# Causal selects of both attentions moved to GpSimd, and half-width scores for the second key block

## The reference, cut to what matters

```python
x = L0_attn_x                                  # (8, 256, 256)
xn = _layernorm(x)
s = mla(xn)                                    # q, k of 16 + 64 per head, rope, causal softmax
#   attn = einsum('bhqd,bhkd->bhqk', q, k) * SCALE;  attn + triu(-inf, k=1);  softmax;  @ v
f = ffn(xn)                                    # mha with 16 per head, the same mask, then
#   x = xn + h @ Wo.T;  + moe(rmsnorm(x)), top 2 of 8 experts
out = x + s * silu(f)
```

## Time and profile before

| | before |
|---|---|
| median of 3 runs | 969.01 us (966.42 to 970.13) |
| the profiled execution | 961.99 us, of which the span from first to last instruction is 960.2 us |
| PE / DVE / ACT / POOL busy | 87% / 68% / 52% / 30% |
| mean granted TensorE clock | 0.952 of full speed |
| one batch of the loop | 77.4 to 77.6 us |

### The profile page before, as it was taken

How to read it: one execution, slowest core, us unless ns; L and a number is a source line. 1 busy time by engine, 2 the same in 40 slices (tenths; PEclk the granted TensorE clock), 3 DMA queues, 4 the chain that set the end, 5 groups by cost and what they waited for, 6 DMA issues and landing times.

```text
span 960.2 us, 20067 instructions
## 1 busy us (share of the span) xinstructions
PE 836.7 (87%) x6688; PEld 747.9 (78%) x6688; DVE 655.9 (68%) x2335; ACT 502.4 (52%) x1091; POOL 285.3 (30%) x282
## 2 busy tenths in 40 slices
PE   5879999999999998999999999977179999999980
PEld 3868988887887797797898788865169999998980
DVE  4877667667767857866866766763237777777754
ACT  2435365365356356446536535634047777676751
POOL 5520310330221131041032023001314565645641
PEclk9988999999999999999999999988579999999995
DMA  9000000000000000000000000030146677779836
GB/s 277 1 1 1 13 1 25 14 1 13 12 11 2 23 11 2 22 12 1 23 12 1 13 16 7 13 141 15 36 151 184 183 238 202 224 232 334 248 49 186
DMA packets 40159, 70.88 MB, mean 74 GB/s; under 512 B 10946, under 2 KB 35138, under 8 KB 37122
## 3 DMA queue, kind: packets, MB, share of 16 engines
q1 hardware_dynamic: 29074, 57.39, 17.7%
q0 software_dynamic: 9856, 12.13, 6.5%
q10 hardware_dynamic: 1152, 0.49, 0.3%
HBM read 55.25 MB, written 14.81 MB: 73 GB/s over the span
## 4 chain that ended last, share of the span: by engine, by line
PE 51%; DVE 14%; DMA 14%; issue 14%; POOL 3%; ACT 2%; SPq 1%; DVEq 0%; POOLq 0%; ACTq 0%
PE ps L575 40%; DMA expert_rows<-yo,slot_of 11%; PE ps L668 6%; PE ps L705 3%; DVE ps L1400 2%; DVE ps L1403 2%; POOL expert_rows L552 1%; DVE negm L1403 1%; PE ps L601 1%; DMA ln<-in_w_ln 1%; DVE negm L1400 1%; POOL xg L541 1%; PE ps L610 1%; DMA xg<-x_normalised,slot_of 1%; PE ps L805 1%
## 5 line engine op out<-in xcount | busy, mean ns | idle before, releaser
L1094 ACT ACTIVATE ex<-ps 128x384 f32<-128x384 f32 x256 | 125.2, 494 | 130.4 <-PE ps L575 128.9
L575 PE MATMUL ps<-qt,kt 128*128 128x256 f32 (+1 forms) x768 | 163.8, 324 | 4.5 <-issue 3.2
L505 POOL TENSOR_TENSOR tok<-tok,swp 128x256 f32<-128x256 f32 x128 | 97.2, 760 | 219.3 <-DVE swp L1355 218.3
L1400 DVE CUSTOM_DVE_ANT_0 ps<-ps,mask 128x128 f32<-128x128 f32 x256 | 76.2, 298 | 70.4 <-PE ps L575 42.6
L1403 DVE CUSTOM_DVE_ANT_0 ps<-ps,mask 128x256 f32<-128x256 f32 x256 | 118.5, 463 | 0.7
L575 PEld LDWEIGHTS ps<-qt,kt 128*128 128x128 f32 x768 | 109.3, 193 | 11.9 <-issue 7.0
L1234 DVE TENSOR_TENSOR wel<-raw,weh 128x768 fp32r<-128x768 f32 x92 | 88.1, 958 | 34.4 <-ACT weh L962 34.4
L552 POOL DMA_INDIRECT expert_rows<-yo,slot_of x46 | 77.9, 1693 | 104.7 <-DMA expert_rows<-yo,slot_of 54.8
L575 PE MATMUL ps<-wh,xth 128*128 128x320 f32 (+2 forms) x352 | 95.5, 353 | 5.9 <-DVE wl L1234 3.3
L1351 DVE TENSOR_TENSOR tok<-ps,cos_t 128x320 f32<-128x320 f32 x128 | 62.7, 490 | 52.3 <-PE ps L575 46.4
L962 ACT ACTIVATE qt<-ps 128x512 f32<-128x512 f32 (+1 forms) x96 | 57.0, 594 | 61.3 <-PE ps L668 54.6
(11 more groups left out here) (164 smaller groups left out, 1965.8 us busy)
## 6 DMA issues: line engine op xcount, KB each, us to landing
raw<-in_w_experts SPq DMA_DIRECT2D x23, 1536.0 KB, 7.2
mla_branch<-s_b SPq DMA_DIRECT2D x8, 256.0 KB, 2.1
expert_rows<-xn SPq DMA_DIRECT2D x8, 256.0 KB, 2.2
x_normalised<-otk SPq DMA_DIRECT2D x8, 256.0 KB, 2.1
xr<-in_x SPq DMA_DIRECT2D x1, 2048.0 KB, 14.8
s_tok<-mla_branch SPq DMA_DIRECT2D x1, 2048.0 KB, 14.2
w_cols_raw<-in_w_cols SPq DMA_DIRECT2D x1, 1792.0 KB, 15.6
x<-expert_rows SPq DMA_DIRECT2D x3, 512.0 KB, 5.1
```

Of the source, the lines that this page charges most:

```text
L505: nc.gpsimd.tensor_tensor(t, t, swp[:, n % 2, :, :], ALU.add).then_inc(tokd, 1)
L575: return nc.tensor.matmul(o, a, m, start=start, stop=stop, skip_group_check=True, **k)
L1094: nc.scalar.activation(ex[:, h % (2 * G), :], ps[4 + h % 2][:, P:4 * P], ACT.Exp, scale=scale).then_inc(ex_, 1)
L1400: nc.vector.tensor_tensor_reduce(out=o[:, 0:P], in0=o[:, 0:P], in1=mask2[:, 1, :], scale=-1.0, scalar=-2.0 * BIG, op0=ALU.add, op1=ALU.min ...
```

## The change

Masking leaves DVE and PE and goes to POOL, for both attentions. POOL runs `affine_select` in place on the same 256 columns of `ex`, once per head: it keeps a value where the query is not before the key and writes 0 elsewhere. `values(g)` of T2 now waits on POOL (`exm2`). `scores2` computes the second key block for queries 128 to 255 alone, and its two mask matmuls go. `power2(b-1)` stands after the select of head 6 in T1, and the four scatters of b-1 stand one each after the selects of heads 9, 10, 11 and 12 of T2. The tiles `seen`, `idb`, `maskb` and the two constants loaded for them go, with two small copies on ACT.

```diff
-            def scatter_slots(r):
-                pool.wait_ge(posd, r + 1)
-                pool.nop(nofuse=True)
-                for t in range(2):
-                    for k in range(2):
-                        nc.gpsimd.indirect_dma_start(slot[:, :], ...
+            def scatter_slot(r, t, k):
+                if t == 0 and k == 0:
+                    pool.wait_ge(posd, r + 1)
+                    pool.nop(nofuse=True)
+                nc.gpsimd.indirect_dma_start(slot[:, :], ...
+            def causal(b, ex_, exm, after):
+                for h in range(H):
+                    wait(pool, ex_, 16 * b + h + 1)
+                    pool.nop(nofuse=True)
+                    a = ex[:, h % (2 * G), 0:2 * P].rearrange("p (a q) -> p a q", a=2)
+                    nc.gpsimd.affine_select(a, a, [[0, 2], [1, P]], ALU.is_ge, zero, 0, -1).then_inc(exm, 1)
+                    after.get(h, lambda: None)()
+            def slots_between(r):
+                return {9 + 2 * t + k: lambda t=t, k=k: scatter_slot(r, t, k) for t in range(2) for k in range(2)}
+            zero = nc.gpsimd.to_reg(0.0)
+            causal(0, ex1, exm1, {})
             rope_sums(1)
+            causal(0, ex2, exm2, {})
             pool.wait_ge(s_slot, 16)
             with pool.Fori(1, last) as b:
-                power2(b - 1)
+                causal(b, ex1, exm1, {6: lambda: power2(b - 1)})
                 rope_sums(b + 1)
-                scatter_slots(b - 1)
-            power2(last - 1)
-            scatter_slots(last - 1)
+                causal(b, ex2, exm2, slots_between(b - 1))
+            causal(last, ex1, exm1, {6: lambda: power2(last - 1)})
+            causal(last, ex2, exm2, slots_between(last - 1))
             power2(last)
...
             def scores2(h, o):
-                mm(o[:, 0:2 * P], kt2[:, h // 2, P:S], qt2[:, h, :], True, False)
-                mm(o[:, 2 * P:4 * P], kt2[:, h // 2, 0:P], qt2[:, h, :], False, False)
-                mm(o[:, P:2 * P], idb[:, :], maskb[:, :], False, True)
-                return mm(o[:, 2 * P:3 * P], idb[:, :], maskb[:, :], False, True)
+                mm(o[:, P:2 * P], kt2[:, h // 2, P:S], qt2[:, h, P:S], True, True)
+                return mm(o[:, 2 * P:4 * P], kt2[:, h // 2, 0:P], qt2[:, h, :], True, True)
...
-                heads(b, scores2, st2, ex2, ex2, pv2, ov2, v2, ...
+                heads(b, scores2, st2, ex2, exm2, pv2, ov2, v2, ...
...
-            def causal(b, h):
-                wait(dve, ex1, 16 * b + h + 1)
-                a = ex[:, h % (2 * G), 0:2 * P].rearrange("p (a q) -> p a q", a=2)
-                nc.vector.tensor_tensor(a, a, seen[:, 0:1, :].broadcast_to([P, 2, P]), ALU.min).then_inc(exm1, 1)
             def stage_m2(b, after):
                 for h in range(H):
-                    causal(b, h)
                     maxima(b, h, (h % 2) * (H // 2) + h // 2, negm2, m2d, mx2)
```

More of the change, by code:

```diff
@@ L56 @@
 BIG = -1e30
-BOUND = 1e30
 IT = FF // P
@@ L92, in build @@
 def build(nc, x, w_cols, w_dq, w_uqr, w_dkv, w_ukv, w_out, w_o, w_ln1, w_ln2, w_r, w_experts,
-          cosines, sines, ident, mask, mask_t, seen_t, upper, route_c, slots, out):
+          cosines, sines, ident, mask, upper, route_c, slots, out):
     ctx = ExitStack()
@@ L171, in build @@
         kt = sb("kt", [P, H, S], F32, early)
-        seen = sb("seen", [P, 1, P], F32, late)
-        idb = sb("idb", [P, P], BF16, late)
-        maskb = sb("maskb", [P, P], BF16, late)
         mask2 = sb("mask2", [P, 2, P], BF16, late)
@@ L513, in power2 @@
                 nc.gpsimd.tensor_tensor(rstd2[:, :], msq2[:, :], mhalf[:, 0:2], ALU.pow).then_inc(rm2, 1)
-            def scatter_slots(r):
-                pool.wait_ge(posd, r + 1)
-                pool.nop(nofuse=True)
-                for t in range(2):
-                    for k in range(2):
-                        nc.gpsimd.indirect_dma_start(slot[:, :], bass.IndirectOffsetOnAxis(posu[:, t, k:k + 1], 0),
-                                                     meta[:, t, k, :], None).then_inc(msc, 16)
+            def scatter_slot(r, t, k):
+                if t == 0 and k == 0:
+                    pool.wait_ge(posd, r + 1)
+                    pool.nop(nofuse=True)
+                nc.gpsimd.indirect_dma_start(slot[:, :], bass.IndirectOffsetOnAxis(posu[:, t, k:k + 1], 0),
+                                             meta[:, t, k, :], None).then_inc(msc, 16)
+            def causal(b, ex_, exm, after):
[9 more added lines that the diff above has]
+            causal(0, ex1, exm1, {})
             rope_sums(1)
+            causal(0, ex2, exm2, {})
             pool.wait_ge(s_slot, 16)
             with pool.Fori(1, last) as b:
-                power2(b - 1)
+                causal(b, ex1, exm1, {6: lambda: power2(b - 1)})
                 rope_sums(b + 1)
-                scatter_slots(b - 1)
-            power2(last - 1)
-            scatter_slots(last - 1)
+                causal(b, ex2, exm2, slots_between(b - 1))
+            causal(last, ex1, exm1, {6: lambda: power2(last - 1)})
+            causal(last, ex2, exm2, slots_between(last - 1))
             power2(last)
-            scatter_slots(last)
+            for t in range(2):
+                for k in range(2):
+                    scatter_slot(last, t, k)
             def gather(blk):
@@ L790, in before_h0 @@
                     wait(pe, v2d, b + 1)
-                heads(b, scores2, st2, ex2, ex2, pv2, ov2, v2, before_h0, lambda: wait(pe, sd, b + 1), max_head,
+                heads(b, scores2, st2, ex2, exm2, pv2, ov2, v2, before_h0, lambda: wait(pe, sd, b + 1), max_head,
                       after)()
@@ L962, in copy @@
                 return nc.scalar.activation(o, a, ACT.Copy)
-            for dst, src in ((idf[:, :], ident), (mask_f[:, 0, :], mask), (mask_f[:, 1, :], mask_t),
-                             (seen[:, 0, :], seen_t), (cos_t[:, :, :], cosines), (sin_t[:, :, :], sines),
+            for dst, src in ((idf[:, :], ident), (mask_f[:, :], mask),
+                             (cos_t[:, :, :], cosines), (sin_t[:, :, :], sines),
                              (up_f[:, :], upper), (rc[:, :], route_c[:, 0:C_OWN])):
@@ L997, in _ @@
                                      scale=ln1[:, m:m + 1]).then_inc(wfh, 1)
-            act.wait_ge(s_k, 16 * 8)
-            copy(idb[:, :], idf[:, :]).then_inc(cast, 1)
-            copy(mask2[:, 1, :], mask_f[:, 0, :])
-            copy(maskb[:, :], mask_f[:, 1, :]).then_inc(cast, 1)
+            act.wait_ge(s_k, 16 * 6)
+            copy(mask2[:, 1, :], mask_f[:, :])
             copy(upb[:, :], up_f[:, :]).then_inc(cast, 1)
@@ L1732, in laid_out @@
     slots[:, 1] = T + np.arange(SLOTS)
-    consts = dict(cosines=cosines, sines=sines, ident=np.eye(P), mask=mask, mask_t=mask.T, seen_t=np.where(i[:, None] > i[None, :], 0.0, BOUND),
+    consts = dict(cosines=cosines, sines=sines, ident=np.eye(P), mask=mask,
                   upper=i[:, None] < i[None, :], route_c=route_c)
```

11 lines of the change are left out of this document (6 added, 5 removed).

## The result

The changed kernel took 973.28 us (median of 10 runs, 969.13 to 978.43), the kernel before 965.53 us beside it (10 runs, 962.62 to 970.13). The ratio is 1.0084, with a 95% interval of 1.0061 to 1.0107: slower by 0.8%.

The account below looks back on a forecast made before the run. PE and DVE were taken to bound T1 and T2 together. T1 -6.3, batch 0's T2 -1.3, T2 of batches 1 to 6 +4.2 and the last T2 +3.9 gave +0.5 on 969.01: 969.5 us, range 957 to 982.

Parts of the forecast that it names:

- The unknown a: Time of one select on POOL, with its wait: 0.62 us taken, range 0.34 to 0.76.
- rival 1: POOL's select takes under 0.51 us, giving 956 to 964 us; faster, chance 0.34.
- T1, -0.9 a batch: T1 without DVE's `min`: PE's waits for DVE shrink 0.9 us in each of batches 1 to 7, -6.3 us.
- T2, the matmuls: PE's T2 head falls from 0.65 to 0.48 us: masks go, plain scores quicken, the narrower score matmul gives nothing.
- T2, the floor of -1.3: Shorter PE heads move DVE's last read in T2 sooner: at best -1.3 us a batch, other end -0.3.
- the formula: Whole change: -29.8 + 49a us; T2 of batches 1 to 6: 7a - 3.64 each; last T2: 7a - 0.4.
- `values(3)` and POOL: In T2 `values(3)` waits for POOL's select of head 15: +4.2 us over batches 1 to 6, +3.9 in the last.
- The rival of the narrow matmul: T2's narrow matmul saves nothing, plain scores stay at 0.32 us: +3.5 us; chance 0.25 within each other case.
- Rival 3, the clock,: PE idles before `values(3)`, its clock falls and P2 loses 1.5 to 3 us a batch: 978 to 987; chance 0.09.
- The diff's scatters: Four scatters among POOL's selects from head 9 of T2, 1.27 us each with the gap, 5.07 in all.

Follow-up runs that it names:

- T2's select only: Changed kernel with DVE's `min` back in T1, so only T2 has selects on POOL: 974.63 us, 1.0085 of the kernel before.
- narrow matmul only: Kernel before, both masks kept, with the first score matmul of `scores2` cut to 128 queries: 970.91 us, 1.0042 of the kernel before.
- T1's select only: Kernel before with only T1's select moved to POOL; T2 and the scatters stay: 971.67 us, 0.9993 of the kernel before.
- before with `project_v2` moved: Kernel before with `project_v2` after head 4 of T2 instead of head 5, nothing else: 959.26 us, 0.9939 of the kernel before.
- early, padded, v2 earlier: Changed kernel with scatters after heads 5 to 7, empty DVE instructions for T1's `min`s, `project_v2` after head 4: 957.84 us, 0.9909 of the kernel before.
- masks on PE: Changed kernel with the old four matmuls of `scores2`, masks included, and POOL's selects kept: 973.19 us, 1.0028 of the kernel before.
- `project_v2` earlier: Changed kernel with `project_v2` after head 4 of T2 instead of head 5: 973.24 us, 1.0013 of the kernel before.
- scatters early: Changed kernel with the four scatters after the selects of heads 5 (two), 6 and 7 of T2: 962.24 us, 0.9971 of the kernel before.
- DVE padded: Changed kernel with an empty DVE instruction, and a wait, where each `min` of T1 stood: 969.28 us, 1.0035 of the kernel before.

## Why the prediction was off, step by step

- **The unknown a** was mis-sized: 0.62 taken, 0.426 measured, inside the bounds of 0.34 and 0.76. The single most awaited number came out as in rival 1, "POOL is quick", and the kernel was still slower. The number of the forecast came out only because this error and those below pull in opposite directions: the smaller a took some 9 us off, the missing terms put some 18 on. The estimate of 0.35 to 0.56 from the Trainium skill (GPSIMD Engine Reference, "Performance pitfalls for Q7 kernels") holds it.
- **T1, -0.9 a batch.** T1 did get 0.85 us shorter, and with the turn restored it reached the end: P2 + T1 fell by 0.7 to 1.0 us a turn in the middle of the loop (28.9 to 29.2 against 29.7 to 30.0). What failed is that the gain was followed only to the end of T1; of P2 the prediction says that the edit doesn't touch it. In P2 the same PE waits for DVE's first cast, and that came later by 0.4 to 1.3 us, first because DVE's shorter code shifted its blocks, then because the scatters had moved to within a microsecond of its branch. Batches 1 to 7 kept 1.3 us of 6.3.
- **T2, the matmuls.** 0.46 us a head against 0.48 forecast, and nothing from width alone: right. The rival of the narrow matmul is out.
- **T2, the floor of -1.3.** It held in batch 0 (-1.1), where there are no scatters and no routing work. In the loop it didn't: PE's freed time ended up in the wait for DVE before head 4, now 1.60 us, and the clock fell on `project_v2` behind it. By the price of one stretch, 1.1 to 1.2 us, six turns cost 7 us, an estimate. Even without a stretch a turn gained only some 0.3 us where the formula with the measured a has 0.7 (47.3, in T2's select only, against 47.5 to 47.6 before).
- **`values(3)` and POOL.** The mechanism and its place were right. In the loop it was hidden by DVE's `negm`. In the last T2 it was +2.6 by the formula with the measured a, and 1.8 us were lost up to the start of `values(3)`. The other 3.9 us came behind it, where the clock was lower for longer. Kernels with no wait for POOL in the last T2 have that too (35.4 to 37.4 us in place of 33.5: narrow matmul only, T1's select only, before with `project_v2` moved, and early, padded, v2 earlier), so it isn't the price of the wait. Moving the scatters alone took all but 0.2 of the loss away; with the padding and the moved projection on top it didn't.
- **Rival 3, the clock,** had 0.09 and was the better part of the truth. It was placed before `values(3)`, where POOL would make PE stand 2.6 us; there PE stood 0.6 to 1.0 us in the loop, and P2 kept its clock in the first trace. It came in the middle of T2, at a wait that already stood in the earlier trace rows with 1.4 us and that the prediction called unchanged, and on the second chip in P2 too, in two of six turns, behind the wait for DVE's cast. The Trainium skill's warning of idle gaps (TensorE: Matmul & The Clock Gate, "Why this matters for your kernels") bears on this place, though the gaps here, 1.4 to 1.6 us, are shorter than the page has them: six of six stretches became two when the gap was filled (early, padded, v2 earlier), and two when PE had its old work back (masks on PE). With the gap filled alone (`project_v2` earlier) four turns still had one. That rival should have been weighed wherever PE waits over 1 us and the edit takes work away ahead of the wait.
- **The diff's scatters** were priced as POOL's time only. As transfers they have neighbours, here the instruction blocks of DVE at the loop's turn. No rival had this, nor that DVE's shorter code moves its blocks. The two share the growth of the turn: it is 3.7 to 4.5 us with both, 3.5 to 3.7 with the scatters early, 3.6 to 3.9 with DVE padded, and 3.0 to 3.3, as before, with both put right. Behind them stand the 5.0 us that batches 1 to 7 lack; the T2 of the loop lacks more, 9.7.

Not settled: why a 1.4 us wait is followed by half clock in some turns and kernels and not in others, why the narrow matmul alone brought stretches, why the clock behind the last T2 differs by kernel, why T1's select alone made two P1 + T2 5.4 us longer, and why a scatter slows an instruction block.

## What to carry to other kernels

A gain in one stage has to be followed to the next place where the same two engines meet; the loop's turn is such a place. Neither busy shares nor waits name it: the profile put the 3.42 us down to PE. Where work is taken from an engine that isn't the bound, it comes to its next wait sooner and stands longer, and on PE that can cost more than the work saved: fill such a gap first, which here gained 0.6% with one moved call. Keep small indirect transfers well ahead of an engine's branch back, and look where the instruction blocks fall after an edit that changes an engine's code length.

## What the runs showed of the hardware

- An in-place select of 128x256 f32 on POOL took 0.426 us on average, 0.39 in a row of three. An indirect scatter of 128 rows takes 0.97 us of POOL, plus 0.17 when a select stands ahead of it; the earlier trace rows have 0.30 between two scatters.
- From DVE's branch back to the head of its loop to its first instruction it was 3.0 to 3.3 us in the kernel before, and up to 4.7 in the others. The 8 KB blocks near it took 0.3 to 0.9 us, or 0.9 to 2.2 within 1.8 us behind a scatter's packets, in the traces of this study, but for the exceptions named above.
- Within one kernel's runs the time rose by 0.2 to 0.3 us for each us at half clock, as fitted for the kernels with 10 runs or more (0.1 for `project_v2` earlier). The changed kernel has some 30 us more of it than before (131 against 98 to 103): by this an estimate of 6 to 9 us, the size of its whole loss. It can't be the whole account, though: `project_v2` earlier and DVE padded have 130 us too, at 1.0013 and 1.0035.
